# A conv loop on 64-column halves of the array, with the high halves of rows doubled by on-chip transfers

## The reference

```
x = (x - mean) / (1e-06 + std) / math.sqrt(P)      # per patch and channel, P = 16
x = _conv2d(x, conv1_w, conv1_b)                   # 3 -> 64 channels, 3x3, 16x16 pixels a patch
residual = x
x = gelu(_group_norm(x, gn1_g, gn1_b))             # 32 groups of 2 channels
x = _conv2d(x, rconv1_w, rconv1_b)                 # 64 -> 64 channels, 3x3
x = gelu(_group_norm(x, gn2_g, gn2_b))
x = residual + _conv2d(x, rconv2_w, rconv2_b)      # linear up to the projection
x = _conv2d(x, proj_w, proj_b, stride=P, pad=0)    # one token of 192 per patch
```

## Time and profile before

| | |
|---|---|
| median of 3 runs | 1872.88 us (1866.81 to 1878.74) |
| the profiled execution | 1862.46 us, its span 1860.6 us |
| PE busy | 1711.3 us (92%), 8824 matmuls |
| DVE busy | 1332.0 us (72%) |
| ACT busy | 944.6 us (51%) |
| POOL busy | 937.2 us (50%) |
| transfers | 124.10 MB, mean 67 GB/s |

### The profile page before, as it was taken

One profiled execution on the slowest core, in us unless ns is written; L12 is line 12 of the kernel. 1 busy time (PEld: TensorE's weight loads), 2 busy tenths in 40 slices (PEclk: granted clock), 3 DMA queues, 4 the chain that ended last, 5 costly groups with the idle time before them and its releaser, 6 DMA issues. The chain is left out here.

```text
span 1860.6 us, 35434 instructions
## 1 busy us (share of the span) xinstructions
PE 1711.3 (92%) x8824; PEld 1082.6 (58%) x8824; DVE 1332.0 (72%) x5077; ACT 944.6 (51%) x2114; POOL 937.2 (50%) x2183
## 2 busy tenths in 40 slices
PE   7899978777999999989998999899999979788999
PEld 2344433333577567747775777477657759655657
DVE  8976767777778878878778878778878864348330
ACT  3466654555555555555555555555555550143441
POOL 2000006676676676666676677676677650133410
PEclk9999989999999999999999999999999989787989
DMA  4442332000222121212211221221122237700000
GB/s 147 145 124 85 90 132 81 19 24 20 70 69 67 46 69 48 65 51 67 67 47 48 67 69 41 75 59 56 42 76 69 65 98 194 157 1 1 1 1 14
DMA packets 51109, 124.10 MB, mean 67 GB/s; under 512 B 9167, under 2 KB 26510, under 8 KB 49062
## 3 DMA queue, kind: packets, MB, share of 16 engines
q1 hardware_dynamic: 50982, 122.52, 22.3%
HBM read 102.76 MB, written 19.69 MB: 66 GB/s over the span
## 5 line engine op out<-in xcount | busy, mean ns | idle before, releaser
L450 PE MATMUL rc<-sb_ghl,sb_rws 128*128 128x512 f16 x3528 | 1057.1, 391 | 20.1 <-ACT sb_g2f L399 17.7
L390 ACT ACTIVATE sb_f32q<-c,sb_gsh,sb_gsc 128x128 f32<-128x128 f32 x788 | 296.2, 456 | 346.0 <-POOL sb_gsh L344 346.0
L450 PEld LDWEIGHTS rc<-sb_ghl,sb_rws 128*128 128x128 f16 x3528 | 343.8, 104 | 161.9 <-issue 38.9
L338 POOL TENSOR_TENSOR sb_tmp<-sb_tmp,sb_half_neg 128x4 f32<-128x4 f32 (+1 forms) x296 | 403.3, 1362 | 23.2
L399 ACT ACTIVATE sb_g2f<-rc,sb_gsh,sb_gsc 128x128 f32<-128x128 f32 x784 | 295.6, 467 | 185.6 <-POOL sb_gsh L344 169.9
L333 POOL TENSOR_TENSOR sb_tmp<-sb_mst 128x4 f32<-128x4 f32 (+1 forms) x296 | 72.5, 245 | 518.1 <-DVE sb_mst L722 515.5
L510 PE MATMUL pj<-sb_wall,sb_arena 128*112 128x384 f16 x896 | 299.3, 341 | 10.1 <-DVE sb_arena L746 8.9
L511 PEld LDWEIGHTS pj<-sb_wall,sb_arena 128*112 128x112 f16 x896 | 243.5, 272 | 90.6 <-issue 3.6
L510 PEld LDWEIGHTS pj<-sb_wall,sb_arena 128*112 128x112 f16 x896 | 243.2, 271 | 40.2 <-DVE sb_arena L746 9.0
L746 DVE TENSOR_TENSOR sb_arena<-sb_g2f,sb_arena 128x512 f32 (+1 forms) x196 | 136.6, 697 | 151.3 <-ACT sb_arena L407 137.6
L511 PE MATMUL pj<-sb_wall,sb_arena 128*112 128x192 f16 x896 | 223.5, 249 | 0.0
(11 more groups left out here) (152 smaller groups left out, 1798.2 us busy)
## 6 DMA issues: line engine op xcount, KB each, us to landing
sb_wall<-w_lo SPq DMA_DIRECT2D x28, 1008.0 KB, 4.9
sb_im<-x_planes SPq DMA_DIRECT2D x300, 60.7 KB
sb_wall<-w_lo SPq DMA_DIRECT2D x14, 1056.0 KB, 4.9
sb_im<-x_planes SPq DMA_DIRECT2D x300, 30.3 KB
sb_f32q<-in_proj SPq DMA_DIRECT2D x12, 576.0 KB, 4.2
sb_arena<-in_proj SPq DMA_DIRECT2D x12, 576.0 KB, 4.7
w_lo<-sb_arena SPq DMA_DIRECT2D x1, 6144.0 KB, 17.1
scratch_fold<-sb_wall SPq DMA_DIRECT2D x24, 247.5 KB
```

The source lines that it names most:

```text
L338: ch.did(gp.tensor_tensor(t5, t3, half_neg[:, 0:w], ALU.pow))
L390: ins = nc.scalar.activation(g1f[:, q * Q + m, :], c1[q][:, m * HALF:(m + 1) * HALF], ACT.Gelu, bias=gsh[q][:, m:m + 1], scale=gsc[q][:, m ...
L450: last = nc.tensor.matmul(out, w[:, wp, 3 * t + m, :], v[:, xp, q * Q:q * Q + Q, t:t + 8, m:m + P], start=(n == 0), stop=(n == 17))
```

## The change

It has six parts.

1. **rconv1 on halves of the array** (`pairs` for `bands`). Each of the 18 full-width matmuls gives way to matmuls of 64 columns that come in pairs: one writes PSUM partitions 0 to 63 (output rows of one parity), the next 64 to 127 (the other). 15 pairs stand in place of 18 matmuls: 6 pairs multiply the low part of the activations by the high weights (`rwl`), then 9 pairs multiply the high part by `rwd`, whose upper 64 rows hold the high weights and whose lower 64 the low ones, so that one pair makes two products.
2. **Doubling.** For those 9 pairs the high part of an activation row must stand in both halves of the partitions. `split1` writes it to a staging tile `hst[q]`, and SP copies it from there into `acts` with four transfers of 64 partitions by 630 f16 per half (`double`). PE waits for them (`s_dup`) after six pairs, ahead of the seventh pair and of `means(0)`.
3. **`split1`** is now one cast and one subtraction of 128x512, in place of three pieces each.
4. **conv1, the group means and the projection** use 64-column halves too: conv1 two matmuls of 64x512, the means two, the projection four matmuls per pixel (token columns 0 to 63 and 48 to 111) in place of two.
5. **Chunks**: 12 of half the size in place of 6; one is loaded after each of the first 12 units of a group, and each is used in two slots.
6. Tokens leave with two stores in place of one, the weights are prepared in other shapes (`rdup` 576 and `rlow` 768 columns for `rbands` 768).

```diff
-NCH = 6
-CHN = [22, 22, 21, 21, 21, 21]
+NCH = 12
+CHN = [11] * 8 + [10] * 4
...
-        ghl = [sb(f"ghl_{i}", [128, 2, U * PAD], F16) for i in range(2)]
+        acts = [sb(f"acts_{i}", [128, 3, HB], F16) for i in range(2)]
+        ghl = [t[:, 0:2, 0:U * PAD] for t in acts]
+        hst = [sb(f"hst_{i}", [128, Q * PAD], F16) for i in range(2)]
...
+            def double(k, p, q):
+
+                sp.wait_ge(s_sp1h, k + 1)
+                for row, half in ((0, 0), (0, 1), (1, 1), (1, 0)):
+                    sp.dma_start(acts[p][64 * half:64 * half + 64, row, q * Q * PAD + WD:(q + 1) * Q * PAD],
+                                 hst[q][64 * row:64 * row + 64, WD:Q * PAD]).then_inc(s_dup[p][q], 16)
+
+            def store_tokens(lo):
+                sp.dma_start(emb[bass.ds(lo, 64), :], tok[0:64, :]).then_inc(s_emb, 16)
+                sp.dma_start(emb[bass.ds(lo + 64, G - 64), :], tok[128 - (G - 64):128, :]).then_inc(s_emb, 16)
...
                         load_im(u + 2, p)
-                    if not first and j < NCH:
-                        load_chunk(g, j)
+                        double(2 * u + 1, p, 1)
+                        double(2 * u + 2, 1 - p, 0)
+                        if not first and 2 * j + p < NCH:
+                            load_chunk(g, 2 * j + p)
...
+            def pairs(out, buf, q):
...
+                low = ((rwl[:, 3 * 2 + m, :], rows(2, 1, m), rwl[:, m, :], rows(2, 1, m)) for m in range(3))
+                edge = ((rwl[:, 3 * 3 + m, :], rows(2, 2, m), rwl[:, 3 + m, :], rows(2, 0, m)) for m in range(3))
+                odd, even = ((1, 1), (0, 1), (1, 2)), ((0, 0), (1, 1), (0, 1))
+                high = ((rwd[:, 3 * ky + m, :], rows(*odd[ky], m), rwd[:, 3 * ky + m, :], rows(*even[ky], m))
+                        for ky in (1, 2, 0) for m in range(3))
+                for n, (w_odd, x_odd, w_even, x_even) in enumerate(itertools.chain(low, edge, high)):
+                    nc.tensor.matmul(out[0:CH, :], w_odd, x_odd, start=(n == 0), stop=(n == 14))
+                    yield nc.tensor.matmul(out[CH:128, :], w_even, x_even, start=(n == 0), stop=(n == 14))
...
-                nc.tensor.matmul(c1[q][:, :], w1s[:, :], v[:, q * Q:q * Q + Q, 0:8, 0:P], start=True, stop=True)
-                nc.tensor.matmul(c1[q][0:CH, :].rearrange("p (g n) -> p g n", g=Q)[:, :, 0:P], w1s[:, 0:CH],
-                                 v[:, q * Q:q * Q + Q, 8, 0:P], start=True, stop=True).then_inc(s_c1, 1)
+                nc.tensor.matmul(c1[q][0:CH, :], w1s[:, 0:CH], v[:, q * Q:q * Q + Q, 1:9, 0:P], start=True, stop=True)
+                nc.tensor.matmul(c1[q][CH:128, :], w1s[:, CH:128], v[:, q * Q:q * Q + Q, 0:8, 0:P],
+                                 start=True, stop=True).then_inc(s_c1, 1)
...
-                woven(8)
+                woven(6)
+                pe.wait_ge(s_dup[p][q], 64 * (pairs_done + 1))
+                woven(1)
                 means(0, N1[q], 2 * u + q + 2, u - (q == 0) if k2 else 0)
-                woven(4)
+                woven(3)
...
-                for half, to, at in parts:
-                    ins = v.tensor_copy(hi[half, :, to, :], src[half, :, at, :])
-                ins.then_inc(s_sp1h, 1)
+                v.tensor_copy(hi, src).then_inc(s_sp1h, 1)
                 dve.wait_ge(s_sp1h, k + 1)
-                for half, to, at in parts:
-                    ins = v.tensor_tensor(lo[half, :, to, :], src[half, :, at, :], hi[half, :, to, :], ALU.subtract)
-                ins.then_inc(s_sp1, 1)
+                v.tensor_tensor(lo, src, hi, ALU.subtract).then_inc(s_sp1, 1)
```

More of the change, by code:

```diff
@@ L16 @@
 from contextlib import ExitStack
+import itertools
 import numpy as np
@@ L168, in build_front @@
         s_g1, s_sp1h, s_sp1 = sem("gelu1_done"), sem("split1_hi"), sem("split1_done")
+        s_rowz = sem("first_rows_zeroed")
+        s_dup = [[sem(f"hi_doubled{p}{q}") for q in range(2)] for p in range(2)]
         s_g2, s_sp2h, s_sp2 = sem("gelu2_done"), sem("split2_hi"), sem("split2_done")
@@ L500, in means @@
                 pe.wait_ge(s_rd[1 - stage_], other + 1)
-                nc.tensor.matmul(st[:, 0:4 * wide[s]], grp[:, :], ms[s][:, :, :, :].rearrange("p a b k -> p (a b k)"),
-                                 start=True, stop=True).then_inc(s_st[stage_], 1)
+                for h in range(2):
+                    last = nc.tensor.matmul(st[64 * h:64 * h + 64, 0:4 * wide[s]], grp[:, 64 * h:64 * h + 64],
+                                            ms[s][:, :, :, :].rearrange("p a b k -> p (a b k)"), start=True, stop=True)
+                last.then_inc(s_st[stage_], 1)
             def project(b, n0, n1):
@@ L509, in project @@
                     both = bass.AP(tensor=wall, offset=n * E, ap=[[WALL, 128], [to_low, 2], [1, E]])
-                    yield nc.tensor.matmul(pj[0:G, 0:2 * E], g2[:, b, 0, :, n], both, start=(n == 0), stop=False)
-                    yield nc.tensor.matmul(pj[0:G, 0:E], g2[:, b, 1, :, n], whi[:, n, :], start=False, stop=(n == HALF - 1))
+                    tiles = ((0, 0), (64, MID))
+                    for at, k in tiles:
+                        last = nc.tensor.matmul(pj[at:at + 64, 0:2 * E], g2[:, b, 0, k:k + 64, n], both,
+                                                start=(n == 0), stop=False)
+                    yield last
+                    for at, k in tiles:
+                        last = nc.tensor.matmul(pj[at:at + 64, 0:E], g2[:, b, 1, k:k + 64, n], whi[:, n, :],
+                                                start=False, stop=(n == HALF - 1))
+                    yield last
             def chunk_waits(g, c):
@@ L522, in emit @@
                 pe.wait_ge(s_g2, 2 * u + q + 1)
-                conv = bands(rc[p][q][:, :], rws, ghl[p], q)
+                conv = pairs(rc[p][q], acts[p], q)
                 proj, c, part = iter(()), 0, 0
                 if s_idx is not None and s_idx >= 4:
-                    c, part = divmod(s_idx - 4, 4)
+                    c, part = divmod(s_idx - 4, 2)
                     if part == 0:
                         chunk_waits(g, c)
-                    lo, hi = (CHS[c] + (CHN[c] * (part + x)) // 4 for x in range(2))
+                    lo, hi = (CHS[c] + (CHN[c] * (part + x)) // 2 for x in range(2))
                     proj = project(1 - b, lo, hi)
-                share = (2 * (hi - lo)) / 18 if s_idx is not None and s_idx >= 4 else 0
+                share = (2 * (hi - lo)) / 15 if s_idx is not None and s_idx >= 4 else 0
                 done = [0, 0]
@@ L542, in woven @@
                             done_proj = run(proj, 1)
-                            if done[1] == 2 * (hi - lo) and part == 3:
+                            if done[1] == 2 * (hi - lo) and part == 1:
                                 done_proj.then_inc(s_pj if c == NCH - 1 else s_pc, 1)
@@ L701, in _ @@
             v.sem_inc(s_sp2, 2)
+            for t in acts:
+                for q in range(2):
+                    v.memset(t[:, 0:2, q * Q * PAD:q * Q * PAD + WD], 0.0).then_inc(s_rowz, 1)
             def channel_stats(stage_, s, src, at):
@@ L800, in _ @@
             read_means(0, 1, 1)
-            split1(0, 0, 0)
+            split1(0, 0, 0, None)
             group(0, 0, True)
```

88 lines of the change are left out of this document (56 added, 32 removed).

## The result

The change makes the kernel slower by 11%: 2082.0 us (2070.7 to 2084.9) against 1871.2 us (1866.8 to 1878.7), a ratio of 1.111 with an interval of 1.105 to 1.117. The forecast was 1980 with a range of 1805 to 2140, so the direction and the mechanism came out as told, and the size is off by a factor of two: 211 us were lost where 107 were expected. That range reaches from a gain to a loss of 14%, so that the time lies in it says little; the range told for this mechanism alone was 1895 to 2120.

The account below looks back on a forecast made before the run. A circle through PE, POOL, ACT and DVE bounds the kernel, not PE. With SP's path deciding, 84 + 8 + 4 + 8 + 4 = +108 us on 1862.5 gave 1970, plus 10 for the median 1980; range 1805 to 2140.

Parts of the forecast that it names:

- PE is not the bound: Main loop before the change: PE's work fills the circle but hardly lengthens it; relieving PE gives next to nothing.
- Pairs run side by side: PE's 64-column matmuls in rconv1: the two of a pair overlap, 0.22 us a pair, 3.3 us for 15.
- rival in series: On PE, pairs run one after another, 2440 us, chance 0.05; or a pair's weight loads don't overlap, some 2000, chance 0.04.
- `split1` saves 0.55 us: DVE's cast and subtraction in one piece: 1.70 to 1.15 us, circle 12.4 in first group, 12.05 in others, 54 us alone.
- The closed path through SP: Means, cast, SP's doublings, chunk, six loads, landing, back to means: 8.56 + 8d us a unit with a chunk, 8.1 + 8d without.
- d, the pitch of a doubling transfer: Time per on-chip transfer of 64 partitions in SP's queue: 0.65 us taken, bounds 0.40 and 0.95.
- The slow copies: Rival: SP's on-chip copies are as slow as `w1s`, d over 0.84: 2090 to some 2215 us, chance 0.14.
- the hidden doubling: Rival: SP's doubling transfers overlap other work, d below 0.45, so the shorter `split1` decides: 1823 us, faster, chance 0.22.
- Group 0: First group, without projection: 14 units at 13.3 us against 12.98 before, 4 us more.
- the circle: Main loop's dependency loop through PE, POOL, ACT and DVE, said to set the unit before: 12.98 us in the first group.
- The unit with a chunk: Main-loop unit that loads a chunk: 13.76 us against 12.6, times 72 units, 84 us more.
- The edges and the last projection: Six edges of groups at 1.3 us each, 8 us; last projection +4, between -15 and +12.

Follow-up runs that it names:

- B: The kernel before the change, unaltered: 1871.2 us; the other runs' ratios are to it.
- A: The kernel after the whole change, against B: 2082.0 us, ratio 1.111.
- both edits: A with the means of norm 1 ahead of PE's doubling wait and each chunk's load a unit later, between the two doublings: 1880.7 us, 1.006 of B.

## Why the prediction was right or wrong, point by point

**PE is not the bound: right.** 129 us less of its work gave at most 13 us.

**Pairs run side by side: right.** Both halves start 0.01 us apart (914.06 and 914.07), and at full clock pairs follow each other at 0.22 to 0.25 us. Neither rival in series has a sign in the profile.

**`split1` saves 0.55 us: right in group 0, too much elsewhere.** 33 us were measured where 54 were told, and units with projection fell to 12.0 to 12.2, by some 0.4. Its cast takes 427 ns and its subtraction 714 (forecast 449 and 697). The step that failed is "to 12.05 in the others" from the first group's saving.

**The closed path through SP: right**, means by means and transfer by transfer. Taking four of the loads out, merging them, moving the chunk and moving the means each moved the time on the side forecast.

**d, the pitch of a doubling transfer: right.** 0.65 was taken from the tail's loads of 64 partitions, another kind of transfer; eight without a pause took 5.03 us (the row at 911.00 above), 0.63 each. That shape and not kind sets it was a guess that held. The slow copies and the hidden doubling both fell with it.

**Group 0: a miss.** 13.3 us a unit was forecast against 12.98 before, and units are 12.3 and 12.4, shorter than before:

```profile
355.06 0.18 DVE L782 TENSOR_REDUCE sb_mst<-st 128x16 f32<-128x32 f32 x1
...
367.33 0.18 DVE L782 TENSOR_REDUCE sb_mst<-st 128x16 f32<-128x32 f32 x1
...
379.73 0.18 DVE L782 TENSOR_REDUCE sb_mst<-st 128x16 f32<-128x32 f32 x1
```

That holds for ten units in the middle of the group, 12.2 to 12.6 us each; its first three and its last take 12.95 to 14.3, and from the first `read_means` of norm 2 to the fifteenth the time is 178.9 us where it was 179.4. Without a chunk the six loads took 4.85 us in place of 5.4 (which was read in a unit with projection), the cast came 0.4 us sooner than summed, and the doublings took 2.4 to 2.5 in place of 2.6, so the path is 12.4 to 12.5 us long. It is still closed there, for PE stands up to 2.7 us for the doubling and DVE 1.8 to 2.0 for the means; it is only little longer than the circle, which with the means moved took 12.2 to 12.3.

**The unit with a chunk: the mis-sized term.** The forecast summed 13.76 us; such units, 71 of the 72 read link by link off the timelines, took 14.99 in the mean (a link runs to the start of the next):

| link | forecast | measured |
|---|---|---|
| means to the end of the cast, SP's start | 1.3 | 0.89 |
| four transfers for half 0 | 2.6 | 2.46 |
| the chunk | 0.46 | 1.52 |
| six loads with gaps | 5.4 | 5.59 |
| four transfers for half 1 | 2.6 | 2.51 |
| landing, from the issue's end | 1.1 | 1.52 |
| one pair and the means | 0.3 | 0.49 |

The step that failed is "the chunk's issue, 0.36 and a gap, 0.46": it counted the issue and left out what the issue waits for, 0.46 us where 1.52 were measured. The kernel's text shows that wait (`s_pc`, which counts the chunks that PE is done with); in B SP has no such wait in its list from 600 to 1400 us. The landing was taken from the store of the tokens, another kind of transfer, and was 0.4 us short; the two together are more than the whole difference. By luck the cast's link was 0.4 us too long in the sum and made up for the landing. Over groups 1 to 6 the loop grew by 207 us where the sum had some 100 for it.

**The clock: not in the prediction at all.** The 0.99 of the loop in B became 0.90. How much of the loss it carries was not isolated. After a long wait it lengthens PE's slot, and with it, by the timeline, the chunk's wait and the last link. Nor is all of that on the path. The clock was 0.89 in group 0 as well (340 to 400 us, against 1.00 in B), and there the links through SP fill the 12.4 to 12.6 us from means to means; so at least without projection the lower clock added next to nothing. When the waits went, it was back at 0.99 without anything being done for it.

**The edges and the last projection: small, as told.** 66.9 us against 64.5 for the projection, forecast +4.

**The Trainium skill's rule** to issue early and wait late ("DMA: Bandwidth & Descriptors", Rules for kernel authors) was weighed as the hidden rival. A did issue as early as its queue let it and waited late, and still lost 211 us; the 910.01 to 928.5 of SP's rows shows why, the transfer was early in the program and late in its queue. With the queue relieved and the means moved, the same transfers, waited for at the same pair, left the kernel at 1849.1 us; early has to be counted from when the queue reaches the transfer.

## What to carry to other kernels

Before a wait for a transfer is put into an engine's in-order queue, sum everything that stands ahead of that transfer in its own queue, issue by issue, and for each of those instructions ask what it waits for itself: a wait that was free while the queue ran ahead is on the path once it does not. Look for closed paths, from an event to the same event one unit on, and cut every one of them; cutting one of two gave 82 and 90 us here, cutting both 201. Then compare what is left with the cheapest part alone: `split1` in one piece, without halves or doubling, took 1827.4 us (with the wrong rows read), less than any variant of the change. And fewer, larger transfers are worth nothing while the queue is idle and 130 us once it is on the path, so read the queue's idle time before spending work on it.

## What the runs showed of the hardware

- An on-chip copy of 64 partitions took 0.59 us to issue, 0.63 from one to the next, and 2.1 us from issue to landing in A (medians, 600 to 1400 us). The landing depends on what else is under way: the median was 2.3 us with four loads, 2.4 with four loads and both edits and 2.5 with both edits alone, and single ones took up to 4.5. A load of 24 or 12 rows took 0.80 and 0.74, and four of 36 or 18 rows some 3.4 together, with gaps. The time of issue hardly follows the bytes: six loads take 5.5 us and four with the same bytes 3.4.
- PE's wait of 4.28 us was followed by a stretch at a granted clock of 0.50, in which a pair took 0.42 us in place of 0.22; the loop's mean clock fell from 0.99 to 0.90 with such waits and came back with them gone. A stall is followed by slower matmuls, then; in the unit above PE still stood 2.11 us for the next doubling, so not all of that slowness was on the path.
- The tail, the same program in all the kernels, took 277 to 278 us in some executions and 284 to 287 in others. The granted clock differs: in five stretches from the last projection on it is 0.72, 0.89, 0.83, 0.89 and 0.99 in B's profiled execution, and 0.77, 0.86, 0.80, 0.85 and 0.95 in A's. B's profiled execution, with the short tail, lay 10 us below B's median; that the tail is the reason isn't shown.
